# The graph stage of a LayerNorm and graph-convolution kernel, rebuilt: counts squared in PSUM, sums and weight products moved

## The chip, the cores and the metric

The kernel runs on one core of one Trainium2 chip. The metric is the device time of one execution, in microseconds; of several runs the median counts. TensorE (PE) multiplies matrices, VectorE (DVE), ScalarE (ACT) and GpSimd (POOL) work element by element, and SyncE (SP) issues all DMAs. They run side by side and are ordered only by semaphores: an instruction that waits holds up everything behind it on its own engine.

## What is computed

```python
def _L0_gnn_ref(x, weight, bias, gumbel):      # x = relu(layernorm(x_in)), weight = adj (128 x 128)
    xp = jnp.transpose(x, (2, 0, 1))           # 1024 nodes, 64 batches, 128 features
    x_avg = xs.mean(axis=1)
    x_norm = x_avg / jnp.maximum(jnp.linalg.norm(x_avg, axis=-1, keepdims=True), 1e-12)
    sim = (x_norm @ x_norm.T + 1.0) * 0.5
    adj = (sim_flat + gumbel[:, 0] > 1.0 - sim_flat + gumbel[:, 1]).reshape(n, n)
    adj_sym = jnp.clip(adj + adj.T, 0.0, 1.0)
    nmask = jnp.clip(adj_sym + jnp.eye(n), 0.0, 1.0)
    common = nmask @ nmask.T
    max_common = common.max()
    struct = jnp.where(adj_sym * (common > 1.0) > 0, common / max_common * common, 0.0)
    W = adj * struct
    deg = W.sum(axis=0)
    dinv = jnp.where(deg > 0, deg ** (-0.5), 0.0)
    Wn = dinv[:, None] * W * dinv[None, :]
    xw = jnp.einsum('nbt,to->nbo', xp, weight)
    return jnp.transpose(jnp.einsum('sd,sbt->dbt', Wn, xw) + bias, (1, 2, 0))
# output = x_in + that, x_in: (64, 128, 1024)
```

## The kernel before

All tiles have 128 partitions; `C` is 8, the number of blocks of 128 nodes. Batches go in 32 pairs. The order of work is written out by hand for each engine.

**First stage.** SP loads the pairs one after the other into eight slots; the load of pair p waits until the relu of pair p-8 is done (`s_h`). DVE takes `bn_stats` of four half rows per pair (L679). For each "four" (two pairs) it aggregates (L640), ACT takes a square root (`std`, L457), and DVE makes `rstd` and `shift` by a chain of six small instructions that are woven into the `bn_stats` of the next four. ACT then writes relu(scale x + shift) (L467). POOL adds the even batches into `hsum` (L407); PE adds the odd ones in PSUM by identity matmuls (L1036). Of every fourth pair PE multiplies both batches by the weight (L1021, 32 matmul records a pair) into banks 2 to 5; ACT copies them out (`keep`, L485), and SP spills them to DRAM in eight groups. On ACT, `std` of four f stands ahead of the relus of four f-1.

**Norm chain.** DVE joins the two sums (L757), ACT squares, PE sums columns (L1044), DVE and ACT make 1/norm of each node, DVE writes it on diagonal tiles (L741, eight of them), PE replicates it by matmuls with ones (L1050), and DVE multiplies. The last two pairs' weight products ("late", four of them) lie between these steps on PE. Meanwhile POOL takes the gumbel differences of row blocks 4 to 7 (L415).

**Graph.** PE makes the similarities (L1077, "dots") through three pairs of PSUM banks; DVE compares them to bf16 `adj` (L775). Transposes and maxima make `nmask` (L780, L783), and ACT counts its rows (L525). PE makes the upper block rows of `common` (L1096). For each block row i, ACT copies the part right of the diagonal as fp16 (`right`, L535), squares the row from PSUM into the SBUF tile `squares` (L539), PE transposes the earlier rows' blocks into place (`left`, L1113), and ACT squares those (L542). DVE masks the diagonal block (L837) and multiplies the row by `adj` into `graph` (L840; the semaphore `s_edge` counts these rows). POOL adds graph rows 0 to 4 into `wide` (L422). DVE adds rows 6 and 7 (L846). PE sums the columns of row 5, of `wide` and of that sum (L1165). Four weight products "ahead" for quad 1 (`ahead`, L1021) lie among these on PE. After the edges DVE makes the outer sums of quad 0 (L800 to L803) and three groups of inner sums (L822 to L827), then the maximum of the counts, which POOL reduces across partitions (L426). DVE and ACT make the inverse root of the column sums, DVE the diagonal tiles, PE replicates them, and ACT copies them to `columns` (L556). From there DVE scales `graph` by rows and columns (L870) and makes the block differences of the two-level Strassen product (L877, L889).

**Quads.** 16 quads of four batches each; a quad is 7 slots of 28 matmul records of 128x256 (L1253). A slot needs its inner sums (`s_comb`) and, in quad 0, its part of the graph (`s_inner`). The last of a slot's four PSUM pieces in slot 0 needs a zeroed bank: `dve.memset(piece(0, 3), 0.0)` (L928), which stands behind all the scaling and `inner_of(2)` on DVE. The factors of quads 2 to 5 come back from DRAM; those of quads 6 to 15 are made during the quad before by `weigh` (L1198): 8 chunks of 8 matmul records, each copied out by ACT.

## Time and profile before

| | us |
|---|---|
| median of 3 runs | 1001.64 (999.19 to 1002.74) |
| the profiled execution | 991.92 |
| its span (first to last instruction) | 990.2 |
| first stage, to the join of the two sums | 0 to 123.1 |
| norm chain, to the first dot | 123.1 to 139.85 |
| dots, masks, first common rows | 139.85 to 170.5 |
| edges, column sums, to the first scaling | 170.5 to 205.5 |
| scaling until slot 2 may start | 205.5 to 230.8 |
| the rest of quad 0 (its end lets SP go on at 275.47) | 230.8 to 275.5 |
| quads 1 to 15 | 275.5 to 981.5 |
| last additions and stores | 981.5 to 990.2 |

All durations are of the one profiled execution. "Idle before" in square brackets names what an engine had waited for. PEclk is the granted TensorE clock, 1.00 for 2.4 GHz and 0.50 for 1.2 GHz. Where an engine waits but does not bound the stage, the wait costs nothing.

### The profile page before, as it was taken

How to read it: one execution, taken by the hardware profiler on the slowest of the kernel's cores; microseconds unless marked ns; L12 is line 12 of the kernel's file. 1: busy time of each engine (PE TensorE's matmuls, PEld its weight loads, DVE VectorE, ACT ScalarE, POOL GpSimd, SP SyncE). 2: the span in 40 equal slices, each digit the busy share in tenths (PEclk: the TensorE clock that was granted, in tenths of full speed). 3: DMA queues.
4: the chain of work that ended last, by engine and by line, in shares of the span. 5: the costliest groups of instructions: out<-in, count | busy, mean ns of one | idle time of the engine just before them, and what ended most of it. 6: DMA issues, size and time to landing. Idle time of an engine off the chain costs nothing.

```text
span 990.2 us, 12614 instructions
## 1 busy us (share of the span) xinstructions
PE 915.1 (92%) x4604; PEld 781.3 (79%) x4608; DVE 740.0 (75%) x1489; ACT 351.2 (35%) x561; POOL 215.6 (22%) x179
## 2 busy tenths in 40 slices
PE   1898889766899999999999999999999999999996
PEld 1555565655788888888888888888888888888885
DVE  6988565997997887978585858585857575757586
ACT  2988716421121212223332424242424242424130
POOL 2877730301021111211111111111111111111111
PEclk9999989777999999999999999999999999999999
DMA  8999870210071633614252525252525252524022
GB/s 347 360 421 401 341 316 1 86 43 1 0 255 33 223 128 128 222 47 179 71 185 72 184 73 182 74 182 74 182 75 181 75 181 76 180 77 179 39 90 85
DMA packets 36264, 149.72 MB, mean 151 GB/s; under 512 B 2800, under 2 KB 2928, under 8 KB 33136
## 3 DMA queue, kind: packets, MB, share of 16 engines
q1 hardware_dynamic: 36208, 148.97, 40.7%
q8 instruction: 35, 0.57, 0.2%
q14 instruction: 21, 0.17, 0.0%
HBM read 107.02 MB, written 41.94 MB: 150 GB/s over the span
## 4 chain that ended last, share of the span: by engine, by line
PE 82%; DVE 9%; ACT 3%; issue 2%; DMA 2%; ACTq 0%; SPq 0%; DVEq 0%
PE ps L1253 66%; PE ps L1198 7%; PE ps L1021 4%; DVE bmem L877 2%; ACT main L467 2%; DVE stats L679 2%; PE ps L1036 2%; DMA main<-in_x 2%; PE ps L1077 1%; DVE bmem L870 1%; PE ps L1096 1%; PE ps L1165 1%; ACT bmem L485 0%; DVE bmem L840 0%; DVE main L741 0%
## 5 line engine op out<-in xcount | busy, mean ns | idle before, releaser
L1253 PE MATMUL ps<-bmem,main 128*128 128x256 f32 x3136 | 697.1, 382 | 18.7 <-DVE ps L928 12.2
L1253 PEld LDWEIGHTS ps<-bmem,main 128*128 128x128 f32 x3136 | 593.8, 192 | 98.6 <-DVE ps L928 12.6
L956 DVE TENSOR_TENSOR main<-ps,main 128x512 f32<-128x512 f32 (+1 forms) x128 | 79.3, 623 | 87.9 <-PE ps L1253 87.9
L439 POOL TENSOR_TENSOR main<-main 128x256 f32<-128x256 f32 x32 | 25.2, 787 | 533.4 <-ACT main L596 533.4
L429 POOL TENSOR_TENSOR main<-main 128x256 f32<-128x256 f32 (+1 forms) x96 | 92.8, 992 | 128.9 <-DVE main L949 128.9
L966 DVE TENSOR_TENSOR main<-main 128x256 f32<-128x256 f32 (+1 forms) x256 | 119.4, 538 | 0.0
L573 ACT ACTIVATE main<-ps 128x512 f32<-128x512 f32 x80 | 47.8, 597 | 201.6 <-PE ps L1198 201.6
L679 DVE BATCH_NORM_STATS2 stats<-main 128x6 f32<-128x512 f32 x128 | 82.3, 673 | 11.2 <-DMA main<-in_x 11.2
L822 DVE TENSOR_TENSOR main<-main 128x256 f32<-128x256 f32 x112 | 47.1, 420 | 54.8 <-PE ps L1253 51.5
L1198 PEld LDWEIGHTS ps<-w_sb,main 128*128 128x128 f32 x640 | 84.0, 192 | 4.1
L564 ACT ACTIVATE ps<-ps 128x512 f32<-128x512 f32 x64 | 33.8, 528 | 149.5 <-PE ps L1253 149.5
L407 POOL TENSOR_TENSOR main<-main 128x1024 f32<-128x1024 f32 x32 | 78.1, 2440 | 39.3 <-ACT main L467 36.8
L1021 PE MATMUL ps<-w_sb,main 128*128 128x128 f32 x384 | 55.6, 311 | 33.1 <-ACT main L467 21.8
L1021 PEld LDWEIGHTS ps<-w_sb,main 128*128 128x128 f32 x384 | 53.5, 225 | 39.8 <-issue 25.2
L1198 PE MATMUL ps<-w_sb,main 128*128 128x128 f32 x640 | 84.3, 275 | 0.0
L467 ACT ACTIVATE main<-main,shift,rstd 128x1024 f32<-128x1024 f32 x64 | 74.1, 1231 | 0.4 <-PE ps L1036 0.4
L564 ACT ACTIVATE main<-ps 128x512 f32<-128x512 f32 (+1 forms) x96 | 50.5, 526 | 64.8 <-PE ps L1253 64.7
L827 DVE TENSOR_TENSOR main<-main 128x256 f32<-128x256 f32 x112 | 61.8, 552 | 3.8
L1036 PE MATMUL ps<-main,ident 128*128 128x512 f32 x128 | 56.3, 592 | 0.0
L825 DVE TENSOR_TENSOR main<-main 128x256 f32<-128x256 f32 x112 | 54.7, 488 | 0.0
L823 DVE TENSOR_TENSOR main<-main 128x256 f32<-128x256 f32 x112 | 54.7, 488 | 0.0
L511 ACT ACTIVATE main<-main,shift,rstd 128x1024 f32<-128x1024 f32 x44 | 54.0, 1231 | 0.0
(95 smaller groups left out, 535.8 us busy)
## 6 DMA issues: line engine op xcount, KB each, us to landing
main<-in_x SPq DMA_DIRECT2D x63, 1024.0 KB, 7.1
out<-main SPq DMA_DIRECT2D x32, 1024.0 KB, 4.9
main<-in_x SPq DMA_DIRECT2D x46, 512.0 KB, 4.6
spill<-bmem SPq DMA_DIRECT2D x8, 1024.0 KB, 8.8
bmem<-in_L_gnn_gumbel SPq DMA_DIRECT2D x8, 1024.0 KB, 12.3
main<-spill SPq DMA_DIRECT2D x8, 1024.0 KB, 6.8
w_sb<-in_adj SPq DMA_DIRECT2D x1, 64.0 KB, 1.8
bias_sb<-in_L_gnn_bias SPq DMA_DIRECT2D x1, 0.5 KB, 2.1
```

Of the source, the lines that this page charges most:

```text
L407: pool.tensor_tensor(hsum[:, :], hsum[:, :], h1[:, k % HPAIRS, 0, :], ALU.add).then_inc(s_even, 1)
L429: pool.tensor_tensor(out_, out_, in_, ALU.add).then_inc(s_pool, 1)
L467: act.activation(h1[:, k % HPAIRS, b, :], xin[:, k % XPAIRS, b, :], ACT.Relu, bias=shift[:, bass.ds(n, 1)], scale=rstd[:, bass.ds(n, 1)]). ...
L564: act.activation(to, from_, ACT.Copy).then_inc(s, 1)
L679: return dve.bn_stats(stats[:, g % 2, c // 2, 6 * f:6 * f + 6], xin[:, k, b, half(f)])
L827: dve.tensor_tensor(s4, q[0, 1], s2, ALU.subtract).then_inc(s_comb, 1)
L956: dve.tensor_tensor(at, piece(slot, b), at, ALU.add).then_inc(s, 1)
L966: dve.tensor_tensor(out_, out_, in_, ALU.add).then_inc(s_low, 1)
L1021: last = pe.matmul(ps[:, first_bank + c // 4, blk(c % 4)], h[:, blk(c)], w_sb[:, :], start=True, stop=True)
L1036: last = pe.matmul(ps[:, f, :], ident[:, :], h1[:, k % HPAIRS, 1, half(f)], start=isinstance(r, int) and k == 0, stop=True, skip_group_che ...
L1198: last = pe.matmul(ps[:, WBANK, blk(c)], hbuf[:, j % HSLOTS, blk(KC * (k % 2) + c)], w_sb[:, :], start=True, stop=True)
L1253: last = pe.matmul(piece(slot, b)[:, QUARTER * e:QUARTER * (e + 1)], left_[:, blk(c)], right_[:, c, :], start=slot in FRESH and b < 3 and ...
```

## The change

- **First stage.** The first three pairs are loaded as single batches. ACT does a small square root at once. The weight product of pair 28 is replaced by that of pair 26, the products stand behind the identity matmuls, and no `keep` is left at the end. Spills begin two pairs later, so four of them instead of five stand ahead of the last load on SP; the gumbel loads stand ahead of four spills. In two places the whole chain to `shift` is done at once. One DVE threshold is moved behind the join.
- **Norm chain.** POOL's differences wait for the last multiply of the chain (`s_unit`). The late products use other banks.
- **Graph.** Counts are squared in place in PSUM; DVE reads the squares there, and the diagonal mask goes into `adj`. The PSUM banks of `common` row i hold row i+3 next, and PE waits for edge i before it writes there. The outer sums of quad 0 and the maximum stand ahead of the edges, the inner sums of slots 0 and 1 go among the compares, those of slot 2 among edges 2 to 5. POOL reduces the maximum first and adds graph rows 0 to 5; PE sums the columns of row 6, `wide` and row 7; DVE's sum of two rows is gone.
- **Quads.** The products ahead are gone; quad 1's factors are made by `weigh` in eight chunks: one ahead of `replicate`, three behind it, four in slots 0 and 1. The memset of `piece(0, 3)` stands ahead of the scaling.

```diff
-    SPILLED = list(range(0, PAIRS, GROUP))
+    SPILLED = list(range(0, PAIRS - GROUP, GROUP)) + [PAIRS - GROUP - 2]
...
-    WEIGHED = range(2 + len(SPILLED) // 2, QUADS)
-    STREAM = [2 * p + b for p in AHEAD + ORDER[2 * WEIGHED[0]:] for b in range(2)]
+    WEIGHED = [1, *range(2 + len(SPILLED) // 2, QUADS)]
+    TURN = {quad: turn for turn, quad in enumerate(WEIGHED)}
+    STREAM = [2 * p + b for quad in WEIGHED for p in ORDER[2 * quad:2 * quad + 2] for b in range(2)]
+    BEFORE, AFTER = (-1, 0), (-1, 1)
+    FIRST_CHUNKS = (BEFORE, AFTER, AFTER, AFTER, (0, 1), (0, 3), (1, 1), (1, 3))
...
-        PSUM3 = (0, 2, 6)
+        def squares(i, c0, c1):
+
+            return bank((0, 2, 6, 4, 2, 6, 4, 2)[i], 2)[:, c0:c1]
+
+        PSUM3 = (6, 2, 4)
...
+                if p < SINGLE:
+                    sp.dma_start(xin[:, p, 0, :], x[2 * p, :, :]).then_inc(s_x_first[p], 16)
+                    sp.dma_start(xin[:, p, 1, :], x[2 * p + 1, :, :]).then_inc(s_x[p], 16)
...
-                if p >= 14 and (p - 14) % GROUP == 0:
-                    spill_group((p - 14) // GROUP)
+                if p >= 16 and p % GROUP == 0:
+                    spill_group((p - 16) // GROUP)
...
-            for g in range(5, KEPT // 2):
+            for g in range(4, KEPT // 2):
...
             def load_h(j):
                 if j >= HSLOTS:
-                    if j - HSLOTS < 4:
-                        sp.wait_ge(s_hw2, j - HSLOTS + 1)
-                    else:
-                        sp.wait_ge(s_chunk, 2 * (j - HSLOTS - 4) + 2)
+                    sp.wait_ge(s_chunk, 2 * (j - HSLOTS) + 2)
...
-            load_h(3)
-            sp.wait_ge(s_left, C)
+            sp.wait_ge(s_left, C - 1)
             load_res(2)
-            for j in (4, 5, 6):
-                load_h(j)
...
@@ -410,20 +403,21 @@
 
 
             pool.wait_ge(s_spill[0], 64)
+            pool.wait_ge(s_unit, 2)
...
-            for i in range(1, C - 3):
+            pool.wait_ge(s_pmax, 1)
+            pool.partition_all_reduce(dmax[:, 1:2], dmax[:, 0:1], 128, RMAX).then_inc(s_gmax, 1)
+
+            for i in range(1, C - 2):
                 pool.wait_ge(s_edge, i + 1)
                 if i > 1:
                     pool.wait_ge(s_colsum, i - 1)
                 pool.tensor_tensor(wide[:, :], graph[:, 0, :] if i == 1 else wide[:, :], graph[:, i, :], ALU.add
                                    ).then_inc(s_colsum, 1)
-
-            pool.wait_ge(s_pmax, 1)
-            pool.partition_all_reduce(dmax[:, 1:2], dmax[:, 0:1], 128, RMAX).then_inc(s_gmax, 1)
...
+            act.activation(dmax[:, 3:4], eps_sb[:, :], ACT.Sqrt)
...
-                    if g % 2 == 1 and (g > 1 or not isinstance(r, int)):
+                    if g % 2 == 0 and (g or not start) or g == 3 and end:
                         for b in range(2):
-                            keep(r * 2 + (g - 3) // 2, b)
+                            keep(r * 2 + (g + 1) // 2 - 1, b)
...
-            rounds(act, PAIRS // XPAIRS, first)
+            rounds_to_last(act, PAIRS // XPAIRS, first)
             relu(XPAIRS - 2, PAIRS - 2, PAIRS // 2 - 1)
             relu(XPAIRS - 1, PAIRS - 1, PAIRS // 2 - 1)
-            keep(ROUNDS - 1, 0)
-            keep(ROUNDS - 1, 1)
...
-            for i in range(C - 1):
+            for i in range(C):
                 count(i)
 
+            def square_right(i):
+                if i < C - 1:
+                    act.wait_ge(s_right, i + 1)
+                act.activation(squares(i, 128 * i, N), squares(i, 128 * i, N), ACT.Square).then_inc(s_csq, 1)
+
+            def square_left(i, j0, j1):
+                act.wait_ge(s_left, i)
+                act.activation(squares(i, 128 * j0, 128 * j1),
+                               ps[:, i % 2, :].bitcast(FP16)[:, 128 * j0:128 * j1], ACT.Square).then_inc(s_lsq, 1)
 
...
-                    act.activation(right[:, RIGHT[i]:RIGHT[i + 1]], counts(i, 128 * (i + 1), N), ACT.Copy
+                    act.activation(right[:, RIGHT[i]:RIGHT[i + 1]], squares(i, 128 * (i + 1), N), ACT.Copy
                                    ).then_inc(s_right, 1)
+                if i < 2:
+                    square_right(i)
+                if i == C - 1:
+                    square_left(i, 0, KC)
+                    square_left(i, KC, i)
+                elif i:
+                    square_left(i, 0, i)
                 if i >= 2:
-                    act.wait_ge(s_edge, i - 1)
-                act.activation(squares[:, i % 2, 128 * i:N], counts(i, 128 * i, N), ACT.Square).then_inc(s_csq, 1)
-                for part, (bank_, j0, j1) in enumerate(left_parts(i)):
-                    act.wait_ge(s_left, i + part)
-                    act.activation(squares[:, i % 2, 128 * j0:128 * j1],
-                                   ps[:, bank_, :].bitcast(FP16)[:, 128 * j0:128 * j1], ACT.Square).then_inc(s_lsq, 1)
-            count(C - 1)
-
-            relu_of(2)
-            take_ahead(0)
-            relu_of(3)
-            take_ahead(1)
+                    square_right(i)
+
             act.wait_ge(s_guard, 2)
             act.activation(node[:, 1, :], node[:, 0, :], ACT.Sqrt).then_inc(s_root, 1)
-            take_ahead(2)
-            take_ahead(3)
-            for f in range(2):
-                act.wait_ge(s_rep, 3 + f)
-                act.activation(columns[:, half(f)], ps[:, 2 + f, :], ACT.Copy).then_inc(s_repc, 1)
...
+            weigh(0, BEFORE)
+            for f in range(2):
+                act.wait_ge(s_rep, 3 + f)
+                act.activation(columns[:, half(f)], ps[:, 1 + f, :], ACT.Copy).then_inc(s_repc, 1)
+            weigh(0, AFTER)
...
+                    at_once = start and g == 1 or end and g == FOURS - 1
...
+                    if at_once:
+                        dve.wait_ge(s_bn, four)
+                        aggregate(g - 1)
+                        long_step(0)
+                        whole_chain(g - 1, four - 1)
+                        for c in range(1, 7):
+                            long_step(c)
...
-            for i in range(GSLOTS - 1):
+            for i in range(GSLOTS - 2):
...
+                inner_sum(0, i // 4, i % 4)
...
+            outer_sums(0)
+            dve.wait_ge(s_cnt, C)
+            dve.reduce_max(dmax[:, 0:1], node[:, 6, :], AX_X).then_inc(s_pmax, 1)
...
-                        diag = squares[:, i % 2, blk(i)]
-                        dve.scalar_tensor_tensor(out=diag, in0=diag, scalar=1.0, in1=diag, op0=ALU.is_gt,
+                        diag = squares(i, 128 * i, 128 * i + 128)
+                        own = adj[:, i, blk(i)]
+                        dve.scalar_tensor_tensor(out=own, in0=diag, scalar=1.0, in1=own, op0=ALU.is_gt,
                                                  op1=ALU.mult).then_inc(s_mask, 1)
                         dve.wait_ge(s_mask, i + 1)
-                    dve.tensor_tensor(graph[:, i, cols], squares[:, i % 2, cols], adj[:, i, cols], ALU.mult
+                    dve.tensor_tensor(graph[:, i, cols], squares(i, cols.start, cols.stop), adj[:, i, cols], ALU.mult
                                       ).then_inc(s_edge, 1)
-
-
-            for f in range(2):
-                dve.wait_ge(s_edge, C + f)
-                dve.tensor_tensor(squares[:, 0, half(f)], graph[:, C - 2, half(f)], graph[:, C - 1, half(f)], ALU.add
-                                  ).then_inc(s_two, 1)
-            outer_sums(0)
-            inner_sums(0, 0)
-            inner_sums(0, 1)
-            inner_sums(0, 2)
-            dve.wait_ge(s_cnt, C)
-            dve.reduce_max(dmax[:, 0:1], node[:, 6, :], AX_X).then_inc(s_pmax, 1)
...
+            dve.wait_ge(s_bits, 1)
+            dve.memset(piece(0, 3), 0.0).then_inc(s_zero, 1)
...
+                    if k < 2:
+                        keep_product(0, k, k)
+                    elif end and k == 3:
+                        keep_product(2, 0, 2)
+                        keep_product(2, 1, 3)
+                    elif not end and k in (4, 5):
+                        keep_product(4, k - 4, k - 2)
...
-            late_times_weight(0, 6)
+            late_times_weight(0, 2)
             pe.wait_ge(s_sq, 1)
-            column_sums(2)
-            late_times_weight(1, 0)
-            replicate(4, 0)
-            pe.wait_ge(s_late, 1)
-            late_times_weight(2, 6)
+            column_sums(6)
+            late_times_weight(1, 4)
+            replicate(6, 0)
+            late_times_weight(2, 0)
             pe.wait_ge(s_unit, 2)
-            pe.wait_ge(s_late, 2)
             for i in range(C):
-                if i == 2:
-                    pe.wait_ge(s_late, 3)
+                if 1 <= i < 3:
+                    pe.wait_ge(s_late, i)
                 if i >= 3:
                     pe.wait_ge(s_adj, i - 2)
                 for f in range(2):
                     last = pe.matmul(ps[:, PSUM3[i % 3] + f, :], hsum[:, blk(i)], hsum[:, half(f)],
                                      start=True, stop=True)
                 last.then_inc(s_dot, 1)
-            pe.wait_ge(s_adj, C - 2)
-            late_times_weight(3, 6)
+            pe.wait_ge(s_late, 3)
+            late_times_weight(3, 0)
...
-                    pe.wait_ge(s_csq, 2 if i < 6 else 3)
+                    pe.wait_ge(s_edge, i - 2)
...
-                if i == 6:
-                    pe.wait_ge(s_csq, 4)
-                    ahead(0)
...
-            for part, source in enumerate((graph[:, C - 3, :], wide[:, :], squares[:, 0, :])):
+            for part, source in enumerate((graph[:, C - 2, :], wide[:, :], graph[:, C - 1, :])):
                 if part == 0:
-                    pe.wait_ge(s_edge, C - 2)
-                if part == 1:
-                    pe.wait_ge(s_csq, C)
-                    ahead(1)
-                    pe.wait_ge(s_colsum, C - 4)
+                    pe.wait_ge(s_edge, C - 1)
+                elif part == 1:
+                    pe.wait_ge(s_colsum, C - 3)
...
-            ahead(2)
-            ahead(3)
-            pe.wait_ge(s_lsq, C)
-            replicate(2, C)
...
+            weigh(0, BEFORE)
+            replicate(1, C)
+            weigh(0, AFTER)
+            pe.wait_ge(s_repc, 2)
```

## Rows read from the trace of the kernel before

**Rows 1.** Windows (us, busy and count by engine, PEclk, DMA share, GB/s).

```profile
20.40:103.30 82.90, 71.86 (x317) 46.86 (x318) 72.88 (x238) 75.57 (x81) 62.46 (x27) 0.98 1.00 393
...
123.10:139.85 16.75, 12.46 (x80) 11.59 (x79) 11.31 (x18) 3.20 (x4) 7.57 (x4) 0.81 1.00 409
139.85:170.50 30.65, 29.70 (x169) 16.96 (x171) 17.03 (x24) 14.10 (x21) 0.00 (x0) 0.99 0.09 37
...
188.00:192.00 4.00, 3.99 (x19) 4.00 (x20) 3.93 (x8) 4.00 (x7) 0.00 (x0) 0.50 0.01 2
...
170.50:205.50 35.00, 26.69 (x194) 24.07 (x193) 32.37 (x54) 17.90 (x31) 9.85 (x5) 0.80 0.24 78
205.50:230.80 25.30, 8.40 (x29) 6.28 (x28) 24.79 (x39) 2.34 (x4) 0.00 (x0) 0.69 0.05 19
230.80:275.50 44.70, 41.87 (x174) 35.70 (x175) 38.13 (x68) 6.51 (x15) 7.24 (x8) 0.91 0.00 0
275.50:981.50 706.00, 705.96 (x3580) 629.70 (x3578) 515.11 (x987) 214.48 (x390) 110.73 (x121) 1.00 0.36 128
```

**Rows 2.** Timeline (start, duration) at the end of the first stage.

```profile
103.31 0.70 DVE L679 BATCH_NORM_STATS2 stats<-main 128x6 f32<-128x512 f32 x1 [1.38 <-DMA main<-in_x]
...
106.77 4.64 ACT L467 ACTIVATE main<-main,shift,rstd 128x1024 f32<-128x1024 f32 x4
...
111.31 1.90 ACT L485 ACTIVATE bmem<-ps 128x1024 f32 x2
112.36 3.84 PE L1021 MATMUL ps<-w_sb,main 128*128 128x128 f32 x32 [1.62 <-ACT bmem L485]
116.04 7.03 PE L1036 MATMUL ps<-main,ident 128*128 128x512 f32 x16
```

**Rows 3.** Timeline of the norm chain, and of the same writes later.

```profile
128.61 1.89 POOL L415 TENSOR_TENSOR bmem<-bmem 128x1024 f32<-128x1024 f32 x1 [8.17 <-DMA bmem<-in_L_gnn_gumbel]
...
130.56 5.01 DVE L741 TENSOR_SCALAR main<-ident,node 128x128 f32<-128x128 f32 x8
...
136.44 3.62 PE L1021 MATMUL ps<-w_sb,main 128*128 128x128 f32 x16
...
202.85 1.66 DVE L741 TENSOR_SCALAR main<-ident,node 128x128 f32<-128x128 f32 x8
```

**Rows 4.** Timeline: VectorE with and without GpSimd beside it.

```profile
172.51 1.23 DVE L840 TENSOR_TENSOR bmem<-main,bmem 128x1024 f32<-128x1024 f32 x1
...
173.82 2.44 POOL L422 TENSOR_TENSOR main<-bmem 128x1024 f32<-128x1024 f32 x1 [36.09 <-DVE bmem L840]
174.09 3.26 DVE L840 TENSOR_TENSOR bmem<-main,bmem 128x1024 f32<-128x1024 f32 x1
...
195.38 0.42 DVE L822 TENSOR_TENSOR main<-main 128x256 f32<-128x256 f32 x1
...
273.85 2.21 DVE L956 TENSOR_TENSOR main<-ps,main 128x512 f32<-128x512 f32 x4
274.02 2.65 POOL L429 TENSOR_TENSOR main<-main 128x256 f32<-128x256 f32 x3 [11.55 <-DVE main L949]
```

**Rows 5.** Timeline: column sums, and the step after the maximum.

```profile
188.01 3.54 PE L1165 MATMUL ps<-ones,bmem 128*128 128x1 f32 x16 [5.39 <-DVE bmem L840]
...
194.91 3.77 PE L1165 MATMUL ps<-ones,main 128*128 128x1 f32 x32
...
200.49 0.16 DVE L857 RECIPROCAL dmax<-dmax 128x1 f32<-128x1 f32 x1 [0.55 <-POOL dmax L426]
```

**Rows 6.** Timeline of the first quad.

```profile
230.83 33.04 PE L1253 MATMUL ps<-bmem,main 128*128 128x256 f32 x140 [12.19 <-DVE ps L928]
...
240.55 0.42 DVE L937 TENSOR_TENSOR main<-ps,main 128x256 f32<-128x256 f32 x1 [5.55 <-PE ps L1253]
...
266.67 33.59 PE L1253 MATMUL ps<-bmem,main 128*128 128x256 f32 x147 [2.79 <-DVE main L956]
```

**Rows 7.** The chain of waits, in order of time: one slot.

```profile
449.00 6.05 PE ps L1253 x28
```

293 lines of the change are left out of this document (137 added, 156 removed).

## Prediction

> **What bounds the kernel now.** I read the windows first: they split the span by what ends each stage [rows 1]. The reader is to see three kinds of stage. Quads 1 to 15, 706.0 us, have PE busy 705.96 at clock 1.00: PE bounds them, and only fewer PE instructions would shorten them. The middle, 123.1 to 275.5, has PE waiting in turns for DVE, ACT and its own clock (0.69 to 0.91). The first stage, 20.4 to 103.3, has the DMA engines at share 1.00, so bytes ahead of the last load set its length. After the last load the timeline shows a serial tail: DVE 103.31, relus 106.77, `keep` 111.31, product 112.36, identity matmuls 116.04 to 123.1 [rows 2].
>
> The edit touches nothing of the steady quads: `weigh` keeps its eight chunks for quads 6 to 15, and the h loads come in the same phase from quad 6 on. All the gain or loss lies before 275.5.
>
> **First stage: -6.2 us.** One spill of 1.05 MB leaves the DMA queue ahead of the last load: at 393 GB/s [rows 1] 2.7 us. The three single loads and the early square root help the start, but DMA bounds what follows; I count 0. So the last pair lands at 100.6 instead of 103.3. From there the tail, with the old durations: statistics and aggregation 2.8 us as before (106.1 - 103.3), 103.4. ACT has to finish the relus of pairs 26 and 27 and two `keep`s first. Their statistics are ready near 97 (two pairs earlier at 2.7 us each, 1.7 us of DVE work), so 97.4 + 4.6 + 1.9 = 103.9. Relus 28 and 29 take 4.6 (to 108.5), the last two `keep`s 1.9 (110.4), relus 30 and 31 4.6 (115.0) [rows 2]. The product of pair 26 waits for `keep`s that end at 103.9 and is done by 106.5, hidden behind relus 28 and 29. The identity matmuls of 28 to 30 are spread over the relus; only those of pair 31 follow, 7.03/4 = 1.8. The join starts at 116.8, not 123.1. Even sums on POOL: the last starts near 114 and takes 2.4, 116.4, just hidden. Bounds: -4 if the DMA queue gives nothing back and POOL comes last; -8.5 if the freer start saves another 2 us of DMA.
>
> **Norm chain: -5.9 us.** The write of the eight diagonal tiles took 5.01 us with POOL's differences beside it, and 1.66 later with POOL idle [rows 3]: 3.35. The tiles began at 130.56, just behind POOL's first difference, 128.61 + 1.89 [rows 3]: the small DVE step before them had waited for it too. Such steps take 0.2 each (twelve between 200.49 and 202.85 [rows 3, 5]); of the 1.89 I take 1.6. PE's late product after `replicate` took 3.62 us at the low clock [rows 3], where 32 records of the first stage take 3.84 [rows 2], so 1.9 for these 16. With the PE gaps closed I expect it at the high clock half of the time: 1.0. Sum 5.95. Bounds -4.5 and -6.7. The moved differences run beside the compares; a compare of row 4 comes five dots later, which is cover for them. The differences' own loads 6 and 7 are issued after the late thresholds but land before that too.
>
> The rule behind this is in the Trainium skill, SBUF — State Buffer, "SBUF: two separate sides": one port pair is an exclusive lock between a GpSimd instruction and a VectorE one with two SBUF inputs or in a two-port mode, and the loser waits for the whole instruction. The row above agrees. It also lets PSUM operands off, which the next part needs; by the opposite rule the sum there would be 6 us worse.
>
> **Dots, masks: 0.** The eight inner sums put among the compares are 0.42 each [rows 4], 3.4 in all, in a stretch where PE is busy 29.70 of 30.65 us and DVE only 17.03 [rows 1]; three bank pairs let a compare be late, also when POOL blocks an inner sum. The last one runs during a late product. Bound +1.
>
> **Edges to first scaling: -1.5 us.** Row by row before: an edge is 1.23 alone, and 3.26 when POOL adds beside it (it starts at 174.09 while POOL holds 173.82 + 2.44, and ends 1.1 after) [rows 4]. Does this hold when one operand is in PSUM? The nearest row is the quads' four additions at 273.85: 2.21 us for three of 512 columns and one of 256, issued under POOL's 2.65 [rows 4], so no blocking. Edges go back to 1.23 and the mask's 0.35 (173.74 to 174.09). But the inner sums of slot 2 have two SBUF inputs, and each now meets a POOL addition: from edge 2 to 5 the pace is 2.44 + 0.42 = 2.9, not 3.5. Against this the outer sums (3 x 1.22) stand ahead and delay the first edge by 1.1, and the count of row 7 delays ACT beside it. Walking this through, the last edge ends 1.1 earlier on the old scale (189.7 for 190.85). Then PE: 48 column sums follow from 188.1, where row 6 is ready. At the low clock 16 cost 3.54, at the high one 32 cost 3.77 [rows 5]; the window has PEclk 0.50 after 5.4 us of idle PE [rows 1, 5]. Three groups are 10.6 low or 5.7 high, so they end at 198.7 or at 193.8. Before they ended at 198.7, and DVE could go on only at 200.49, after the all-reduce [rows 5]; that wait of 1.8 goes, since the maximum is long done. I take the low clock: the weight product that stood between the column sums is gone, and nothing but 1-column matmuls is left to keep PE active. `replicate` at the low clock and the chunk ahead of it give back about 0.3. Hence -1.5, with bounds -6.5 (clock high from 188) and +3 (edges coupled through the reused banks at the old pace, and column sums low).
>
> The Trainium skill, TensorE: Matmul & The Clock Gate, "What's actually happening", says that the throttled state is the default and sustained activity releases it; it speaks against taking products out of this chain, and the row at 188 agrees. It would not change the sum, which already goes by the low clock.
>
> **Quad 0: -6.5 us.** PE waited 12.19 us for the memset at 230.83 and ran slots 0 (tail) and 1 only after all scaling; DVE in turn waited 5.55 us at 240.55 for slot 1 [rows 6]. With the memset early, slots 0 and 1 (6.05 us each [rows 7]) and four chunks (0.96 each, half of the 1.9 above) fit into the 25.3 us of scaling: start at +5.7, or +7.7 when the three chunks ahead run low, 7.7 + 12.1 + 3.8 + some 3 of low clock gives at most +26.6. Slot 2 starts at +25.3 to 26.5 instead of +32 to 35. From then on DVE is the bound: its work from 230.8 to the last addition before 266.67 was 35.9 less the 5.55 of waiting. The stall of 2.79 at 266.67 stays, since it is DVE's end that sets it [rows 6]. So quad 0 ends 5.6 us earlier by DVE, and up to 1.8 more if the clock does not fall during the shorter wait; I take -6.5. Bounds -4 (slot 2 late by the chunks and their relus, which wait for h loads) and -7.5.
>
> **Sum.** -6.2 - 5.9 + 0 - 1.5 - 6.5 = -20.1; 991.9 - 20.1 = 971.8 on the profiled execution. The median of the runs shown is 1.0% above that execution, for which I have no row; the gain carried over gives 1001.6 - 20.1 = 981.5. Ends of the terms: -29 and -7.5.
>
> **Rivals.**
> - *Clock high through the column sums* (chance 0.13): the denser graph stage keeps PE granted. For it: the second column-sum group ran at 3.77 for 32 [rows 5]. Against: that came right after a 128-column product. It gives another -5, and -1 at `replicate`: 975.5.
> - *POOL still blocks DVE with a PSUM operand, or the reused banks bind* (0.15): edges keep their 3.3 each and the inner sums come on top, 4 x 1.5 = +6, and PE waits for edges with each common row. 987.5. Only the additions at 273.85 speak against it.
> - *The first stage stays DMA bound* (0.07): the tail is hidden by a later landing, since gumbel loads now stand in the same queue; -2 instead of -6.2, and POOL last: 986.
> - *Slower* (0.04): PE stays at the low clock from the column sums through slots 0 and 1. The place is slot 0's start; 56 slot records cost 12.1 more, seven chunks 6.7 more and `replicate` 1.8 more, 20.6 in all, which is what the edit gains; it decides once slot 2 starts 20 us after the scaling is done. PE at 0.69 in that stage before speaks a little for it [rows 1], the continuous work against it. 1003.
> - *Nothing moves* (0.03): DMA and the PE gap lengths shift but quad 0 waits for the same DVE end; within 0.3%.
> - The forecast itself 0.58, own range 977 to 986.
>
> **How the numbers follow.** 0.3% (3 us) is about what a measurement can tell from no change. Faster: 0.58 + 0.13 + 0.15 + 0.07 = 0.93; same 0.03; slower 0.04. The range 972.5 to 992.5 holds the forecast, the first three rivals and the -29 and -10 ends; 0.1 to 0.15 is left out.
>
> **What would show it.** Right: the join (`hsum` from PSUM) near 117 and the last load at 100 to 101; the eight diagonal tiles at 1.7 us and the first dot 10 to 12 us after the join; edges at 1.2 us beside POOL, with slot 2's inner sums at 2 us and more; three column-sum groups at 3.5 us each; PE in slots 0 and 1 during the scaling, no 12 us wait; quad 1 starting near 60 to 64 us after the first scaling, where it was 70; 706 us for quads 1 to 15. Wrong: an edge above 3 us, PE waiting on `relu` in front of a chunk, a stall of ACT on an h load in quad 0, or more than 706 us in the steady quads.

## Result and the profile after

The changed kernel takes 975.26 us (median of 4 runs, 972.77 to 981.56) against 1000.41 for the kernel before on the same chip (4 runs, 994.55 to 1002.74): a ratio of 0.9759, 95% interval 0.9724 to 0.9794, or 25.2 us less. The prediction was 981.5 with a range of 972.5 to 992.5, and 977 to 986 for its own mechanism. Most steps hold in the profiles; behind the last statistics they make 16.6 to 17.3 us. The rest of the 25.2, some 8 us, lies ahead of them, where the prediction had 2.7 us, and its cause is not settled.

The two profiled executions differ by 10.4 us only (991.92 and 981.56): that of before is faster than all its four timed runs, that of after the slowest of its four. So a table of stages comes first, each read from the starts of the named instructions in the timeline, for every kernel of the study (us). The first column is the start of the last statistics aggregation (VectorE), which follows the last load of x; "join" is the addition of the two sums into `hsum`. Quad 1 is counted from the end of quad 0 on PE, where SP issues its next load (275.47 in before, 264.02 in after).

| kernel | last aggregate at | to the join | to the first dot | to the first scaling | to quad 1 | to the end | span |
|---|---|---|---|---|---|---|---|
| before | 106.1 | 17.0 | 16.7 | 65.7 | 70.0 | 714.7 | 990.2 |
| before_again | 114.0 | 17.2 | 16.7 | 65.8 | 70.0 | 714.7 | 998.4 |
| after | 112.2 | 14.1 | 9.9 | 64.8 | 63.1 | 715.8 | 979.8 |
| after_again | 106.0 | 14.1 | 9.9 | 63.8 | 63.2 | 715.8 | 972.8 |
| first_only | 113.4 | 14.8 | 13.4 | 65.7 | 70.2 | 714.8 | 992.3 |
| rest_only | 111.0 | 18.6 | 9.9 | 64.7 | 63.0 | 715.8 | 982.9 |
| pool_early | 106.6 | 15.2 | 15.7 | 64.6 | 63.1 | 715.9 | 981.0 |
| memset_late | 105.7 | 14.1 | 9.9 | 65.0 | 71.9 | 714.7 | 981.3 |
| reduce_last | 108.7 | 14.1 | 9.9 | 63.1 | 64.8 | 714.7 | 975.2 |
| filler | 104.7 | 15.2 | 11.2 | 63.3 | 63.2 | 715.8 | 973.4 |
| sums_out | 110.1 | 14.1 | 11.2 | 63.8 | 63.2 | 715.9 | 978.3 |
| all_three | 107.2 | 14.1 | 11.2 | 59.6 | 63.2 | 715.8 | 971.1 |
| spills_behind | 100.8 | 15.3 | 12.9 | 64.4 | 63.2 | 715.8 | 972.2 |
| best | 103.1 | 15.4 | 11.2 | 62.3 | 63.0 | 715.8 | 970.9 |

The columns behind the join repeat within 0.2 us between before and before_again. Between after and after_again they do too, but for the way to the first scaling, 64.8 and 63.8: the matmuls of `replicate` ran at the low clock in the one (3.16 us) and at the high one in the other (1.95). The first column moves by 8 us between two executions of the same kernel. One profile can judge a stage behind the join, not the loads.

Windows of after, by stage (us, busy and count of PE, PE's weight loads, DVE, ACT, POOL, PEclk, DMA share, GB/s); they answer to [rows 1]:

```profile
126.33:136.35 10.02, 9.40 (x81) 9.04 (x80) 7.48 (x19) 3.20 (x4) 0.93 (x1) 1.00 0.95 364
136.35:167.64 31.29, 30.29 (x173) 17.05 (x175) 24.57 (x37) 15.91 (x23) 6.70 (x4) 1.00 0.30 120
167.64:200.96 33.32, 25.47 (x134) 20.78 (x135) 19.56 (x44) 11.09 (x24) 12.10 (x6) 0.64 0.10 32
200.96:226.50 25.54, 19.54 (x117) 17.42 (x115) 25.10 (x38) 12.04 (x18) 1.26 (x1) 0.97 0.19 62
226.50:264.00 37.50, 33.46 (x140) 28.12 (x140) 36.46 (x65) 5.40 (x12) 5.04 (x4) 0.93 0.00 1
264.00:970.00 706.00, 705.16 (x3576) 629.40 (x3577) 516.17 (x989) 212.46 (x388) 112.24 (x123) 1.00 0.36 129
```

The norm chain (first line) was 16.75 us at clock 0.81 and is 10.02 at 1.00. During the scaling (fourth) PE is busy 19.54 us, where it had 8.40. The edges and column sums (third) are hardly shorter, and their clock fell from 0.80 to 0.64. The 706 us of steady quads are what they were.

Timeline of after (start, duration, engine, line, what; in brackets the idle time before and what ended it), from the tail of the first stage to quad 1:

```profile
113.27 4.63 ACT L462 ACTIVATE main<-main,shift,rstd 128x1024 f32<-128x1024 f32 x4
...
114.41 4.54 DVE L755 TENSOR_TENSOR bmem<-bmem 128x1024 f32<-128x1024 f32 x2
114.58 11.57 POOL L400 TENSOR_TENSOR main<-main 128x1024 f32<-128x1024 f32 x4 [1.65 <-ACT main L462]
...
117.81 1.91 ACT L482 ACTIVATE bmem<-ps 128x1024 f32<-128x1024 f32 x2
...
119.62 4.64 ACT L462 ACTIVATE main<-main,shift,rstd 128x1024 f32<-128x1024 f32 x4
...
124.31 1.98 PE L1044 MATMUL ps<-main,ident 128*128 128x512 f32 x4 [0.28 <-ACT main L462]
...
126.33 1.23 DVE L763 TENSOR_TENSOR main<-ps,main 128x1024 f32<-128x1024 f32 x1 [7.38 <-PE ps L1044]
...
132.17 1.66 DVE L747 TENSOR_SCALAR main<-ident,node 128x128 f32<-128x128 f32 x8
...
134.40 1.95 PE L1029 MATMUL ps<-w_sb,main 128*128 128x128 f32 x16
...
135.42 1.90 POOL L409 TENSOR_TENSOR bmem<-bmem 128x1024 f32<-128x1024 f32 x1 [9.26 <-DVE main L772]
...
167.86 0.38 POOL L413 PARTITION_ALL_REDUCE dmax<-dmax  x1 [24.81 <-DVE dmax L846]
...
171.40 3.60 PE L1109 MATMUL ps<-bmem 128*128 128x512 bf16 x8 [0.41 <-DVE bmem L860]
...
175.49 2.33 POOL L419 TENSOR_TENSOR main<-bmem 128x1024 f32<-128x1024 f32 x1 [7.25 <-DVE bmem L860]
177.97 9.82 POOL L419 TENSOR_TENSOR main<-main,bmem 128x1024 f32<-128x1024 f32 x4
178.10 2.49 DVE L816 TENSOR_TENSOR main<-main 128x256 f32<-128x256 f32 x1
...
180.83 1.23 DVE L860 TENSOR_TENSOR bmem<-ps,bmem 128x1024 f32<-128x1024 f32 x1
...
184.69 3.54 PE L1160 MATMUL ps<-ones,bmem 128*128 128x1 f32 x16 [4.84 <-DVE bmem L860]
188.10 3.55 PE L1160 MATMUL ps<-ones,main 128*128 128x1 f32 x16
191.51 3.55 PE L1160 MATMUL ps<-ones,bmem 128*128 128x1 f32 x16
...
256.81 7.17 PE L1237 MATMUL ps<-bmem,main 128*128 128x256 f32 x32 [2.91 <-DVE main L964]
264.83 5.42 PE L1237 MATMUL ps<-bmem,main 128*128 128x256 f32 x24 [0.85 <-DVE main L964]
```

What it shows, in order. The tail of the first stage belongs to ACT (relus and `keep`s without a gap from 113.27 to 124.26) and to PE's last identity matmuls behind it, which end at 126.29 and release the join. POOL's four additions end at 126.15, just hidden; of the 7.03 us of identity matmuls on PE behind the last relu [rows 2] the last pair's are left. The diagonal tiles take 1.66 us instead of 5.01 [rows 3], since POOL's first difference now starts behind them, and the late product runs at 1.95, the high clock, instead of 3.62. An edge with a PSUM operand takes 1.23 us while POOL adds (180.83 lies inside 177.97 to 187.79); it took 3.26 [rows 4]. An inner sum with two SBUF operands is the one that waits now: of the four of slot 2 the first two take 0.41, the third 2.49 and the fourth 1.11. The column sums are at the low clock, three groups of 3.5. PE no longer waits 12.19 us in quad 0 [rows 6]; one wait of 2.91 is left, as before.

Two things were not foreseen. POOL's first graph addition starts 7.25 us after the all-reduce, although its edge had been ready for 4 us. And quad 1 meets a new wait of 0.85 us for the additions of quad 0's last slot.

### The profile page after: what moved, and what is told of

Its sections match the earlier page's. It is cut to its first block, busy times and chain, and to the rows that moved or that the text cites. A ratio compares the mean times of both kernels' runs of the same rounds, so it can differ in the third digit from the quotient of the medians.

```text
span 979.8 us, 12545 instructions
## 1 busy us (share of the span) xinstructions
PE 916.6 (94%) x4604; PEld 777.9 (79%) x4608; DVE 728.9 (74%) x1487; ACT 353.4 (36%) x566; POOL 218.1 (22%) x180
## 4 chain that ended last, share of the span: by engine, by line
PE 80%; DVE 9%; ACT 4%; DMA 4%; issue 2%; ACTq 0%; SPq 0%; DVEq 0%
PE ps L1237 66%; PE ps L1177 7%; DMA main<-in_x 4%; ACT main L462 3%; DVE bmem L888 3%; DVE stats L688 2%; PE ps L1090 1%; PE ps L1029 1%; DVE bmem L881 1%; PE ps L1160 1%; PE ps L1109 1%; PE ps L1044 1%; ACT bmem L482 1%; DVE bmem L860 1%; DVE bmem L900 0%
## 5 line engine op out<-in xcount | busy, mean ns | idle before, releaser
L564 ACT ACTIVATE main<-ps 128x512 f32<-128x512 f32 x88 | 52.6, 597 | 211.7 <-PE ps L1177 211.7
L1177 PEld LDWEIGHTS ps<-w_sb,main 128*128 128x128 f32 x704 | 93.1, 193 | 6.6 <-issue 1.2
L688 DVE BATCH_NORM_STATS2 stats<-main 128x6 f32<-128x512 f32 x128 | 82.0, 674 | 20.5 <-DMA main<-in_x 20.5
L1044 PE MATMUL ps<-main,ident 128*128 128x512 f32 x128 | 64.6, 639 | 34.1 <-ACT main L462 34.0
L1177 PE MATMUL ps<-w_sb,main 128*128 128x128 f32 x704 | 93.8, 277 | 1.6 <-ACT main L564 1.6
L811 DVE TENSOR_TENSOR main<-main 128x256 f32<-128x256 f32 x112 | 48.6, 434 | 54.2 <-PE ps L1237 50.9
L1044 PEld LDWEIGHTS ps<-main,ident 128*128 128x128 f32 x128 | 23.5, 200 | 61.6 <-issue 40.9
L819 DVE TENSOR_TENSOR main<-main 128x256 f32<-128x256 f32 x112 | 62.5, 558 | 3.7
L816 DVE TENSOR_TENSOR main<-main 128x256 f32<-128x256 f32 x112 | 56.8, 507 | 0.0
L813 DVE TENSOR_TENSOR main<-main 128x256 f32<-128x256 f32 x112 | 55.3, 494 | 0.0
L1029 PEld LDWEIGHTS ps<-w_sb,main 128*128 128x128 f32 x320 | 40.4, 199 | 9.7 <-issue 9.7
```

What stands on the lines that cost most here:

```text
L688: return dve.bn_stats(stats[:, g % 2, c // 2, 6 * f:6 * f + 6], xin[:, k, b, half(f)])
L816: dve.tensor_tensor(s2, s1, q[0, 0], ALU.subtract).then_inc(s_comb, 1)
L819: dve.tensor_tensor(s4, q[0, 1], s2, ALU.subtract).then_inc(s_comb, 1)
L1044: last = pe.matmul(ps[:, f, :], ident[:, :], h1[:, k % HPAIRS, 1, half(f)], start=isinstance(r, int) and r == k == 0, stop=True, skip_grou ...
L1177: last = pe.matmul(ps[:, WBANK, blk(c)], hbuf[:, j % HSLOTS, blk(KC * (k % 2) + c)], w_sb[:, :], start=True, stop=True)
```

## The experiments

**first_only and rest_only** split the change. first_only is the kernel before with the first stage of after: the order of loads and spills, which pair is spilled last, `keep` and its product spread over the relus.

```
-    SPILLED = list(range(0, PAIRS, GROUP))
+    SPILLED = list(range(0, PAIRS - GROUP, GROUP)) + [PAIRS - GROUP - 2]
...
-                if p >= 14 and (p - 14) % GROUP == 0:
-                    spill_group((p - 14) // GROUP)
+                if p >= 16 and p % GROUP == 0:
+                    spill_group((p - 16) // GROUP)
```

rest_only is the rest of the change without it.

> The kernel before with the first stage of the change alone (single first loads, four spills ahead of the last load, pair 26 in place of 28, products behind the identity matmuls, no keep at the end). Theory 1, the tail after the last load is shorter and one spill is out of the way: 6 to 12 us faster than before (about 991), with the join of the two sums 13.5 to 16.5 us after the last load's first statistics, where the kernel before needs 19.8. Theory 2, the first stage as a whole gains nothing, as the two profiled executions alone would say (the join came 3.2 us later): within 2 us of before, or slower. In both the stages behind the join last as before: 16.7, 65.7 and 70.0 us.

> The changed kernel with the first stage of before. What the profile of the changed kernel showed behind the join: norm chain 10.0 us instead of 16.75, first dot to first scaling 64.6 instead of 65.7, quad 0 63.1 instead of 70.0, and 1.0 lost ahead of quad 1: 13.6 us faster than before, about 987. Theory 1 then wants the two halves to add up to the 25 us of the whole change; theory 2 wants this kernel to carry all of the gain, 975.

Measured: first_only 995.09 us against 1000.87, ratio 0.9943 (0.9921 to 0.9965), 5.8 us less; rest_only 986.18, ratio 0.9837 (0.9805 to 0.9869), 14.7 less. In first_only the tail is 2.2 us shorter, and the norm chain 3.4: POOL's differences meet it at another point, and the diagonal tiles take 3.30 us instead of 5.01. That makes 5.6, all of what was measured; nothing is left for the loads. The expectation for first_only missed in three places: the gain is just under its 6 to 12 us, the join came 17.3 us behind the last pair's first statistics and not 13.5 to 16.5, and the norm chain did not stay at 16.7. In rest_only the stages behind the join have their full gains, and the tail is 1.6 longer. Neither theory holds as written: the halves add up to 20.5 of the 25.2, and the 3.4 of the norm chain stands in both halves.

**before_again and after_again** are the two kernels unedited, each profiled once more.

> The kernel before once more, for a second profile of its first stage. If the DMA rate differs from execution to execution, the last load lands elsewhere than at 103.3 us and everything behind the join keeps its length to 0.3 us. If the first stage is bound by ACT and PE, it repeats 103.3 to 0.5 us.

> The changed kernel once more. Theory 1: the last load lands some 6 us before the 109.6 us of the first profile (this execution was the slowest of four), near 103, and the join follows 16.7 us later. Theory 2: it lands near 109.6 again.

Measured: 1000.16 and 974.51 us. The last aggregate moved from 106.1 to 114.0 in the one and from 112.2 to 106.0 in the other. One window of the loads shows why (columns as above), in after:

```profile
60.00:80.00 20.00, 17.75 (x69) 10.96 (x70) 15.95 (x53) 14.48 (x16) 13.10 (x6) 0.83 0.98 353
```

and in after_again:

```profile
60.00:80.00 20.00, 17.44 (x81) 11.28 (x80) 18.67 (x62) 16.80 (x19) 14.68 (x7) 0.91 1.02 420
```

The DMA engines are busy nearly all the time in both, and move 353 or 420 GB/s. Over the 80 us from 20 to 100 it is 360 and 387, and 362 and 391 in the two executions of before. A rate 7 or 8% lower over some 100 us is what the last aggregate moved by.

**pool_early** lets POOL's differences start as before.

```
             pool.wait_ge(s_spill[0], 64)
-            pool.wait_ge(s_unit, 2)
```

> The changed kernel, with GpSimd's four gumbel differences no longer held back until the norm chain is over. If they cost the chain by blocking DVE (theory), the eight diagonal tiles take 4 to 5 us again and join to first dot is 13 to 15 us, not 9.9. Rival: the chain is shorter for its other banks and order, and stays at 9.9 with the differences beside it, or because the gumbel loads land later than the chain in this kernel.

Measured: 982.7 us, join to first dot 15.66 us instead of 9.86. Its timeline:

```profile
124.76 4.30 POOL L408 TENSOR_TENSOR bmem<-bmem 128x1024 f32<-128x1024 f32 x2 [3.52 <-DMA bmem<-in_L_gnn_gumbel]
...
127.29 1.80 DVE L740 TENSOR_SCALAR node<-node 128x8 f32<-128x8 f32 x1
...
129.33 3.30 DVE L746 TENSOR_SCALAR main<-ident,node 128x128 f32<-128x128 f32 x8
129.62 1.95 POOL L408 TENSOR_TENSOR bmem<-bmem 128x1024 f32<-128x1024 f32 x1 [0.55 <-DMA bmem<-in_L_gnn_gumbel]
...
134.42 3.18 PE L1028 MATMUL ps<-w_sb,main 128*128 128x128 f32 x16
```

A step of 0.17 us becomes 1.80, the tiles 3.30, and the late product falls to the low clock (3.18 for 1.95). The one wait is worth 5.8 of the 6.9 us. The expectation had 13 to 15 us for the stage and 4 to 5 for the tiles; the stage came out longer and the tiles shorter, with 1.6 for the small step and 1.2 for the late product beside them.

**memset_late** puts the clearing of slot 0's piece back behind the scaling.

```
             diagonal()
-            dve.wait_ge(s_bits, 1)
-            dve.memset(piece(0, 3), 0.0).then_inc(s_zero, 1)
             dve.wait_ge(s_rows, 1)
...
+            dve.wait_ge(s_bits, 1)
+            dve.memset(piece(0, 3), 0.0).then_inc(s_zero, 1)
+
             def finish(quad, j):
```

> The changed kernel with the memset of piece(0, 3) back behind all scaling. Theory: PE waits at the end of slot 0 for it again, slot 1 comes after the scaling and DVE waits for slot 1: first scaling to quad 1 is 69 to 70 us, not 63.1. Rival: the sums made earlier and the missing products ahead gave the gain, and it stays within 1 us of 63.1.

Measured: 983.02 us, scaling to quad 1 71.88 instead of 63.1. PE again waits for the memset:

```profile
204.77 1.89 PE L1238 MATMUL ps<-bmem,main 128*128 128x256 f32 x8
220.01 2.08 PE L1238 MATMUL ps<-bmem,main 128*128 128x256 f32 x4 [13.35 <-DVE ps L937]
```

So two moved lines are worth 8.8 us there, less the 1.05 that the quads behind get back (714.7 for 715.8), 7.7 in all: no less than all that quad 0 gained. It is 2 us more than the 69 to 70 that were expected, and more than the 70.0 of the kernel before.

**reduce_last** moves `partition_all_reduce` behind the additions of the graph.

```
-            pool.wait_ge(s_pmax, 1)
-            pool.partition_all_reduce(dmax[:, 1:2], dmax[:, 0:1], 128, RMAX).then_inc(s_gmax, 1)
-
             for i in range(1, C - 2):
...
+            pool.wait_ge(s_pmax, 1)
+            pool.partition_all_reduce(dmax[:, 1:2], dmax[:, 0:1], 128, RMAX).then_inc(s_gmax, 1)
+
             def add(out_, in_, count):
```

> The changed kernel with GpSimd's reduction of the maximum behind its graph additions instead of ahead. In the changed kernel the first addition began 7.3 us after the reduction, 4.1 us after its second edge was there, in three profiles alike (7.25, 7.43, 7.35). Theory A, GpSimd has to get other code after the reduction: the first addition follows the second edge within 0.2 us, the fifth ends about 4 us earlier. Theory B, GpSimd waits for the port that DVE holds with its edge rows: the first addition begins late as before. First dot to first scaling changes little in either (64.7 less 0 to 1), since 48 column sums at the low clock follow.

Measured: 976.94 us. POOL's timeline:

```profile
167.91 2.34 POOL L416 TENSOR_TENSOR main<-bmem 128x1024 f32<-128x1024 f32 x1 [28.37 <-DVE bmem L860]
170.39 2.35 POOL L416 TENSOR_TENSOR main<-main,bmem 128x1024 f32<-128x1024 f32 x1
173.24 7.32 POOL L416 TENSOR_TENSOR main<-main,bmem 128x1024 f32<-128x1024 f32 x3 [0.50 <-POOL main L416]
186.39 0.38 POOL L420 PARTITION_ALL_REDUCE dmax<-dmax  x1 [5.82 <-issue]
```

The addition starts with its edge; the fifth ends 47.9 us behind the first dot, where it was 51.6. Now the all-reduce starts 5.8 us after the last addition, with its input long ready and nothing recorded between them. The time lies between the two kinds of instruction, not in a port or a semaphore. The first scaling came 63.1 us behind the first dot, 0.8 or 1.7 below the two executions of after, where 0 to 1 was expected. The Trainium skill, GPSIMD Engine Reference, "2.1 Instruction dispatch", gives about 6 us for the first call of a freshly loaded kernel, with no instruction in the profile; the 5.8 us agree with it in size, and nothing in the trace shows what the engine does in them. The page speaks of no price on the way back to an ordinary addition; the row of after has one, 7.25 us.

**filler** puts 20 matmuls of 512 columns, whose result nobody reads, ahead of the column sums.

```
             pe.wait_ge(s_lsq, C - 2)
+            for _ in range(20):
+                pe.matmul(ps[:, 0, :], nmask[:, 0, 0:128], nmask[:, 0, half(0)], start=True, stop=True)
```

> The changed kernel with 20 matmuls of 512 bf16 columns, whose result nothing reads, in PE's pause ahead of the column sums (bank 0). Theory, the column sums run at the low clock because PE had paused: the first 16 take 1.9 instead of 3.5 us, the 48 take 5.7 to 9 instead of 10.4, except that GpSimd's last addition, which ends 3 us after they begin, holds the second group up; first dot to first scaling falls by 2 to 4 us. Rival: the column sums are slow for themselves (weight loads of one-column products), and nothing changes, or the filler delays them.

Measured: 975.12 us. PE's timeline:

```profile
174.78 4.49 PE L1153 MATMUL ps<-bmem 128*128 128x512 bf16 x20
179.39 1.95 PE L1162 MATMUL ps<-ones,bmem 128*128 128x1 f32 x16
182.63 3.58 PE L1162 MATMUL ps<-ones,main 128*128 128x1 f32 x16 [1.29 <-POOL main L419]
186.06 3.55 PE L1162 MATMUL ps<-ones,bmem 128*128 128x1 f32 x16
```

The first group runs at the high clock, then PE waits for POOL's last addition and the next groups are low again. Of the 5 us that a high clock would be worth, 1.6 appear in the first group, and the wait takes 1.3 of them. The theory missed here: the 48 column sums take 10.2 us and not 5.7 to 9, and the first scaling comes 0.5 or 1.4 us earlier, not 2 to 4.

**sums_out** takes the four inner sums out of the loop of the edges, into VectorE's 9 us of waiting; **all_three** adds the edits of reduce_last and filler to it.

```
-                if 2 <= i < 6:
-                    inner_sum(0, 2, i - 2)
 
+            inner_sums(0, 2)
             dve.wait_ge(s_gmax, 1)
```

> The kernel after with one edit: the four inner sums of slot 2 leave the loop of the edges (where two of them took 2.49 and 1.11 us beside GpSimd's adds instead of 0.41) and stand behind the last edge, in the 9 us in which VectorE waits for the column sums. Theory A: GpSimd's adds, which begin 7.3 us after its partition_all_reduce, are what the second group of column sums waits for, so VectorE's blocked sums lie beside that wait: the first group starts some 3 us earlier and the second stays at about 55 us... that is, within 0.5 us of where it was (51.8 us behind the first dot); from the first dot to the first scaling 63.8 to 64.8 us as in the two executions of after. Theory B: the blocked sums are the path (my prediction's high bound had them there): the first group and all behind it move up by 3 to 4.4 us and the scaling comes at 60 to 61.5.

> sums_out with two more edits of this study: partition_all_reduce behind GpSimd's adds, and 20 matmuls of 512 columns ahead of the column sums. With theory A the three wait on one another, and only together do they pay: VectorE's loop ends some 3 us earlier, GpSimd's adds end with it, the first group runs at the high clock (1.95 us for 3.54), the second does not wait. From the first dot to the first scaling 59.5 to 61.5 us (64.8 and 63.8 in the executions of after, 63.1 for each of the two edits alone); the maximum from partition_all_reduce, ready 5.8 + 0.4 us behind the last add, comes before the last column sum. Time 970 to 973, some 3 us below after; ratio to the kernel before 0.969 to 0.974. Theory B (VectorE alone was the path): sums_out alone would already have given 3 to 4 us and this one adds only the 1.6 of the clock.

Measured: sums_out 979.99 us (one run), first dot to first scaling 63.80, inside the two executions of after. Its first group of column sums is early (44.9 us behind the first dot) and the second waits 3.32 us for POOL. all_three 973.14 us (970.72 to 978.58), ratio 0.9743 (0.9708 to 0.9779), first dot to scaling 59.60:

```profile
178.04 1.84 PE L1161 MATMUL ps<-ones,bmem 128*128 128x1 f32 x16
180.52 1.95 PE L1161 MATMUL ps<-ones,main 128*128 128x1 f32 x16 [0.65 <-POOL main L416]
182.33 2.77 PE L1161 MATMUL ps<-ones,bmem 128*128 128x1 f32 x16
...
186.20 0.38 POOL L420 PARTITION_ALL_REDUCE dmax<-dmax  x1 [5.73 <-issue]
186.61 0.16 DVE L865 RECIPROCAL dmax<-dmax 128x1 f32<-128x1 f32 x1 [5.06 <-POOL dmax L420]
```

Theory A holds in this profile. VectorE's blocked sums, POOL's late additions and PE's clock lie side by side: one at a time the edits gave 0 to 1.7 us up to the first scaling, together 4.2 to 5.2 (against either execution of after). It is one execution: in best, below, the same three edits gave 1.6 to 2.5. In one point the expectation missed: the maximum came after the last column sum, not before. The sums end at 185.10 and VectorE goes on at 186.61, when the all-reduce is done, so its switch costs 1.5 us of the path here. The time is at the upper end of what was expected: the norm chain took 1.4 us more than in after, at a clock of 0.85. Its interval overlaps that of after, so the times alone don't show a gain.

**spills_behind** issues the four spills that stand between the loads behind the last load; **best** is all_three with it.

```
-                if p >= 16 and p % GROUP == 0:
-                    spill_group((p - 16) // GROUP)
 
+            for g in range(4):
+                spill_group(g)
             for i in range(GSLOTS):
                 load_gumbel(i)
```

> The kernel after with one edit, the prediction's DMA term four times over: the four spills of 1.05 MB that still stand between the loads of x on SP's queue are issued behind the last of them, ahead of the first gumbel loads. Theory A (bytes ahead of the last load set its time): 4 x 1.05 MB at 350 to 390 GB/s are 10.8 to 12 us, but ACT and VectorE, busy 88 and 87% of that stretch in the kernel before, take over as the bound at some 2.7 us a pair; the last aggregate comes 7 to 10 us earlier, at 96 to 104 (after and its kin: 104.7 to 112.2), the thresholds wait for the same bytes as ever (near 115 to 119), and the join follows by 112 to 117: a time of 967 to 971. Theory B (the rate of the transfers, which moved by up to 20% from one execution to the next, or ACT and VectorE set the stage): the aggregate stays within 104 to 114 and the time within 3 us of after's 975.

> all_three with the spills behind the last load as in spills_behind. The two lie in different stages, so their gains add: all_three is at 973.1; theory A of the first stage gives 965 to 969 (ratio to the kernel before 0.964 to 0.969), theory B 971 to 975. The stages behind the join take what they take in all_three: 9.9 or 11.2 us to the first dot, 59.6 to the first scaling, 63.2 to quad 1, 715.8 from there.

Measured: spills_behind 974.01 us (973.48 to 976.39), ratio 0.9743 (0.9705 to 0.9782); best 971.00 (969.19 to 972.61), ratio 0.9705 (0.9667 to 0.9743). The last aggregate came at 100.8 and 103.1, earlier than in any of the twelve other profiles, with ACT busy 76.37 and 74.70 of the 80 us from 20 to 100 (67.89 and 72.56 in the executions of after). The bytes do count. Whether ACT limits what they give, or the rate does (362 and 348 GB/s in that window), is not shown. But both times stayed at theory B's. The timeline of spills_behind says where the gain went:

```profile
109.19 1.23 DVE L755 TENSOR_TENSOR bmem<-bmem 128x1024 f32<-128x1024 f32 x1 [6.10 <-DMA bmem<-in_L_gnn_gumbel]
109.58 6.35 POOL L400 TENSOR_TENSOR main<-main 128x1024 f32<-128x1024 f32 x2 [1.54 <-ACT main L462]
111.64 2.08 DVE L755 TENSOR_TENSOR bmem<-bmem 128x1024 f32<-128x1024 f32 x1 [1.23 <-DMA bmem<-in_L_gnn_gumbel]
...
120.69 3.76 PE L1029 MATMUL ps<-w_sb,main 128*128 128x128 f32 x16
124.24 3.04 PE L1065 MATMUL ps<-main,ones 128*128 128x128 f32 x16
```

The thresholds now meet POOL's last additions (6.35 us for two; two at a time took 4.86 before them), which costs 1.2 in the tail, and the norm chain falls to the low clock and takes 3.0 more. In best the way from the first dot to the first scaling took 62.3 us and not the 59.6 of all_three: the edges began 33.2 us behind the first dot instead of 31.5, the matmuls of `common` row 4 took 2.62 for 1.90, and the column sums, without any wait, 1.84, 2.49 and 3.55. best is the fastest kernel of the study, some 4 us below after; the intervals of the two ratios still overlap, and against all_three the further gain is not shown.

## Why the prediction held, step by step

| step | predicted | measured in the profiles |
|---|---|---|
| first stage, loads | -2.7 | not settled, between 0 and -8 |
| first stage, tail | -3.6 | -2.9 behind the last aggregate |
| norm chain | -5.9 | -6.9 |
| dots, masks | 0 | +0.8 |
| edges to first scaling | -1.5 | -1.7 (-2.6 in after_again) |
| quad 0 | -6.5 | -6.9 |
| quads 1 to 15 | 0 | +1.05 |
| sum behind the last aggregate | -17.5 | -16.6 (-17.3) |

That the time fell into the range owes something to luck. It lies outside the 977 to 986 that the prediction gave its own mechanism, and next to the 975.5 of the rival with the high clock, which did not come. With the forecast 2.7 us for the loads and the measured steps behind them it would be about 981; the 5.5 us more have no cause on record. The prediction also added its bounds wrongly: they give -29 and -8.5, not -7.5 or -10.

**First stage, tail: right, 0.7 short.** ACT and then PE end it, as worked out, and POOL is just hidden: beside two thresholds its four additions take 11.57 us, not the 9.6 of their free price, and end 0.14 before PE. In first_only, spills_behind and best POOL does come last. The 0.7 are in two places: ACT starts on relus 28 and 29 1.0 behind the start of the last aggregate, not 0.5, and the last identity matmuls with what stands around them take 2.1, not 1.8. Seen from the landing of the last load the tail gains less, 1.8 to 2.5 us: VectorE was ready for it before (2.8 to the aggregate), and in after it is still at the pair before (3.2 and 3.9).

**First stage, loads: the step that is not settled.** The stages behind the last aggregate repeat to about 1 us, so the median times tell where it stood: the time less 1.7 us outside the span, less the row of the stage table. That gives 114.6 for before (1000.41 - 1.7 - 884.1), 114.5 for first_only, 112.6 for rest_only, 106.4 for after (the mean of its two rows) and 107.5 for all_three. So in first_only the new loads gave nothing over the kernel before, and in after and all_three 5 to 6 us over rest_only, with the same code in the first stage. This difference is no larger than what one execution differs from another (8 us), and the interval of the whole ratio is 7 us wide. Removing four more spills took it to about 101, 5.5 us less where bytes alone would give 10.8. I had 2.7 for one spill, and the last load at 100.6; it landed at 109.1 and 102.0. The bytes are a real price, but its size in this edit is not shown, nor why after stands 8 us earlier than first_only. What the prediction treated as one rate, 393 GB/s [rows 1], lies between 353 and 420 in the same window of the same kernel.

**Norm chain: right, and only the clock's share was mis-sized.** The tiles 3.35 and the small step 1.6, as worked out; the late product gave its whole 1.7 (3.62 to 1.95), where I took 1.0 as "half of the time". pool_early shows that these three belong to one wait. The clock is not certain there: in five kernels with edits elsewhere it fell, and the chain took 11.2 to 12.9 us.

**Dots, masks: +0.8**, inside the bound of +1: the three outer sums stand ahead of the first edge, which I had booked with the next stage. Both stages together give -0.9 and -1.8, against -1.5.

**Edges to first scaling: the sum right, the account incomplete.** Edges at 1.23 beside POOL, low column sums, the wait for the maximum gone, the last edge 1.1 us earlier behind the first dot: as forecast. Of the inner sums all four were to be blocked; in after two were (2.49 and 1.11), in after_again one (1.11), because POOL began late. Not in the account were POOL's 7.25 us behind the moved all-reduce, which set the second column-sum group (2.08 us of PE's waiting in after_again), and the common rows of row 4, which ran at the low clock in both executions (3.60 and 3.31 us where all_three has 1.90), after PE had paused for the first edges. I asked what the all-reduce waits for and not what it leaves behind on POOL. In the kernel before its switch lay inside a 13 us wait, and nothing showed it. The rival of a high clock did not come. In filler the one-column groups lost it again behind a wait for POOL, and in best without any wait. The rival of a PSUM operand that is blocked is refuted by the row at 180.83; by the Trainium skill, SBUF — State Buffer, "SBUF: two separate sides", a VectorE instruction with at most one SBUF input, outside the 2-port modes, does not contend with GpSimd, and the row's 1.23 us agrees. The reused banks bound little: PE had to wait for the first edge before its transposes, which held VectorE up for 0.62 us ahead of the second (169.79), and ahead of row 4 of `common` it waited 0.41.

**Quad 0: right.** Slots 0 and 1 run inside the scaling and slot 2 starts 25.6 us after it began, within 25.3 to 26.5 (34.8 in before). The 2.9 us wait stayed. memset_late shows the cause.

**Quads 1 to 15: right that they are untouched, but +1.05 ahead of them.** PE reaches quad 1 earlier than VectorE has finished the additions of quad 0 (0.85 at 264.83); memset_late and reduce_last, in which PE comes later, have 714.7 again. A part of what quad 0 gains is given back where VectorE is next: PE's first record of quad 1 comes 63.9 us behind the first scaling, where it was 69.8, and from there to the end it is 715.0 and 714.9.

## What to carry to other kernels

Where a custom GpSimd instruction moves among ordinary ones, count 6 us ahead of it and 7 behind it and put it where that engine has nothing due; its own 0.4 us is not its price. These kernels run it once each, so whether a second one would pay again is not shown. When three engines finish a stage side by side, an edit for one of them measures little (0 to 1.7 us here): list who is late next, and edit them together. And before a change of a few us in a DMA-bound stage is judged, profile the same kernel twice: here its rate alone moved the stage by 8 us.

## What the runs showed that was not expected

- Between `partition_all_reduce` and an ordinary addition POOL was idle for 7.0 to 7.7 us in all eight profiles with this order, and for 5.7 to 5.8 in the other direction (reduce_last, all_three, best), with the semaphores met for the last 4 us of the first and all of the second.
- The first stage moved 353 or 420 GB/s in the same 20 us of the same kernel, with a DMA share of 0.98 and 1.02, and 360 or 387 over 80 us.
- Groups of 16 one-column matmuls in f32, each with its own weight load, kept PE busy 10.37 of 10.61 us at a granted clock of 0.50 in after. Behind 20 matmuls of 512 columns they ran at 1.95 us and fell back to 3.55 within the next group; in all_three, with a wait of 0.65 us between, two groups stayed at the high clock and the third took 2.77; in best, without a wait, they took 1.84, 2.49 and 3.55.
